# Layer 0 of a two-layer kernel: one multiply by C over two neighbouring PSUM banks instead of two over one bank each

## The reference, cut to what matters

```python
A = -jnp.exp(A_log[0])
dA = jnp.exp(delta[..., None] * A[None, :, None, :])
dBu = (delta * u)[..., None] * Bs[:, None, :, :]
...
_, states = jax.lax.associative_scan(comb, (dA, dBu), axis=2)
y = jnp.einsum('bdln,bln->bdl', states, Cs) + D_param[0][None, :, None] * u
```

## Time and profile before

| | us |
|---|---|
| median of 3 executions | 3519.16 |
| profiled execution, its time | 3515.45 |
| profiled execution, its span | 3513.4 |
| PE busy in the span | 3303.4 (94%) |
| DVE busy | 2848.3 (81%) |
| ACT busy | 2436.5 (69%) |
| POOL busy | 2366.1 (67%) |
| L1052 (`times_c`), 768 operations | 487.6 |

### The profile page before, as it was taken

One profiled execution on the slowest core, in us unless ns is written; L12 is line 12 of the kernel. 1 busy time (PEld: TensorE's weight loads), 2 busy tenths in 40 slices (PEclk: granted clock), 3 DMA queues, 4 the chain that ended last, 5 costly groups with the idle time before them and its releaser, 6 DMA issues. The chain is left out here.

```text
span 3513.4 us, 38815 instructions
## 1 busy us (share of the span) xinstructions
PE 3303.4 (94%) x10616; PEld 1690.2 (48%) x10616; DVE 2848.3 (81%) x4084; ACT 2436.5 (69%) x4194; POOL 2366.1 (67%) x1566
## 2 busy tenths in 40 slices
PE   5967999999999999999999999997989999999998
PEld 2422343434334343443433434342347877777887
DVE  7799999999999999999999999998733355565532
ACT  3688888888888888888888888886535565433211
POOL 3399999999999999999999999999800001022111
PEclk9987999999999999999999999998999999999999
DMA  9444555565555655555565555646442233366654
GB/s 381 152 106 98 142 150 145 149 168 140 155 143 151 165 148 152 145 150 155 141 168 139 160 140 152 168 119 186 108 117 69 63 99 107 121 212 212 213 185 157
DMA packets 213736, 529.89 MB, mean 151 GB/s; under 512 B 25144, under 2 KB 46328, under 8 KB 208272
## 3 DMA queue, kind: packets, MB, share of 16 engines
q1 hardware_dynamic: 170512, 376.39, 33.4%
q0 software_dynamic: 43008, 151.02, 20.0%
HBM read 346.17 MB, written 80.48 MB: 121 GB/s over the span
## 5 line engine op out<-in xcount | busy, mean ns | idle before, releaser
L554 PE MATMUL p_in<-xn,win_v 128*128 128x512 f32 (+1 forms) x2160 | 976.7, 600 | 50.6 <-ACT halo L825 30.5
L570 PE MATMUL p_op<-uy,wout_ring 128*128 128x512 f32 x2160 | 975.5, 601 | 23.6 <-DVE x_res L1083 23.5
L1018 POOL TENSOR_TENSOR g_ring<-du,bc 128x2048 f32<-128x2048 f32 x192 | 870.8, 4535 | 15.1
L1046 DVE TENSOR_TENSOR_SCAN p_da<-p_da,state,g_ring 128x512 f32<-128x512 f32 x672 | 827.4, 1277 | 42.4 <-issue 28.7
L1069 DVE SCALAR_TENSOR_TENSOR p_cv<-win_v,conv_w,p_cv 128x512 f32<-128x512 f32 x960 | 723.1, 753 | 47.5 <-ACT p_cv L883 26.5
L554 PEld LDWEIGHTS p_in<-xn,win_v 128*128 128x128 f32 x2160 | 402.9, 192 | 594.1 <-issue 592.4
L570 PEld LDWEIGHTS p_op<-uy,wout_ring 128*128 128x128 f32 x2160 | 404.8, 191 | 581.5 <-issue 543.5
L764 ACT ACTIVATE p_da<-delta,A 128x512 f32<-128x512 f32 x768 | 500.0, 683 | 12.8 <-ACT state L769 0.4
L1052 DVE TENSOR_TENSOR g_ring<-p_da,bc 128x512 f32<-128x512 f32 x768 | 487.6, 677 | 0.0
L1524 PE MATMUL banks<-x_split,w_split 128*128 128x512 f32 x1152 | 458.1, 398 | 12.6 <-DVE x_split L1727 6.7
L1526 PE MATMUL banks<-x_split,w_split 128*128 128x512 f32 x1152 | 450.0, 391 | 0.0
(11 more groups left out here) (250 smaller groups left out, 4176.1 us busy)
## 6 DMA issues: line engine op xcount, KB each, us to landing
g_ring<-g_ring POOLq DMA_DIRECT2D x192, 512.0 KB, 5.2
win_v<-in_win SPq DMA_DIRECT2D x192, 384.0 KB, 3.1
wout_ring<-wout_scratch SPq DMA_DIRECT2D x184, 384.0 KB, 4.1
x_ring<-x_scratch SPq DMA_DIRECT2D x192, 256.0 KB, 2.7
q_scratch<-q_ring POOLq DMA_DIRECT2D x96, 256.0 KB, 2.5
x_split<-q_scratch SPq DMA_DIRECT2D x96, 256.0 KB, 3.4
out<-x_ring POOLq DMA_DIRECT2D x96, 256.0 KB, 2.9
x_res<-in_x SPq DMA_DIRECT2D x90, 256.0 KB, 4.6
```

Source lines behind the costliest of these rows:

```text
L554: last = nc.tensor.matmul(bank_in(i)[:, 0:n], WR[:, i % NW, t, :], XN[:, t, off:off + n], start=(t == 0), stop=(t == XT - 1))
L570: last = nc.tensor.matmul(p_op[:], OR[:, e % NO, k - h * HALF, :], ucol(c * K + k), start=(k == 0), stop=(k == K - 1))
L1018: nc.gpsimd.tensor_tensor(G[:, i % NG], DU[:].unsqueeze(1).broadcast_to([P, NS, N]), BB[:], ALU.mult).then_inc(s_dbu, 1)
L1046: nc.vector.tensor_tensor_scan(bank, bank, G[:, i % NG, n, :], init, ALU.mult, ALU.add)\
```

## The change

`times_c` now takes a pair p of states instead of one state n. It waits for the second scan of the pair, reads both banks of `p_da` and two neighbouring parts of `CB`, writes two neighbouring parts of the `G` slot, and counts `s_cm` up by 2. The four calls in a slot become two. No other engine's waits or order change.

```diff
-                def times_c(i, n):
-                    vec.wait_ge(s_scan, NS * i + n + 1)
-                    vec.wait_ge(s_c[n // 2], 16 * (i // K + 1))
-                    nc.vector.tensor_tensor(G[:, i % NG, n], p_da[:, n % 2, :], CB[:, n], ALU.mult).then_inc(s_cm, 1)
+                def times_c(i, p):
+                    vec.wait_ge(s_scan, NS * i + 2 * p + 2)
+                    vec.wait_ge(s_c[p], 16 * (i // K + 1))
+                    nc.vector.tensor_tensor(G[:, i % NG, 2 * p:2 * p + 2], p_da[:], CB[:, 2 * p:2 * p + 2], ALU.mult)\
+                      .then_inc(s_cm, 2)
...
                         scan(a, 0)
                         scan(a, 1)
                         times_c(a, 0)
-                        times_c(a, 1)
...
                         scan(a, 2)
                         scan(a, 3)
-                        times_c(a, 2)
-                        times_c(a, 3)
+                        times_c(a, 1)
```

## The result

| | before | after |
|---|---|---|
| median of the executions, us | 3519.49 (4) | 3556.72 (4; 3553.14 to 3557.37) |
| span of the profiled one | 3513.4 | 3554.6 |
| idle time of VectorE's scans in the steady part | 14.4 | 3.1 |

The ratio is 1.0105, with an interval from 1.0091 to 1.012: 37 us slower. (The kernel before has one more execution here than where the forecast starts from, 3519.16.) The forecast was 3530, 11 us slower, with a range to 3545. The sign was right, and so was the view that VectorE becomes the pace; the price of a pair was too low by half, and a term of it was missing.

A forecast was written before the change was run, and what follows sets the result against it. The prediction took PE with its ScalarE answers to set 150 us a chunk in layer 0. Steady part 8.2, head 1.0 and tail 1.5 sum to 10.7 us, added to 3519.2 for a forecast of 3530, range 3516 to 3545.

The forecast's parts named there:

- the price of a pair: Layer 0, second scan to the operation behind the products: 1.16 us against 1.09, so VectorE loses 0.07 us a pair.
- What bounds the kernel: Layer 0's steady part: PE with its ScalarE answers sets 150 us a chunk; VectorE has about 1.0 us to spare.
- the cover: VectorE's idle time in layer 0's steady part, 14.4 us, about 1.0 us a chunk, which absorbs added VectorE time.
- The start: Wide product behind the second scan: starts 0.04 us after its end instead of 0.09 before, losing 0.13 us a pair.
- The length: Wide product on VectorE: 512 more columns cost 0.53 us, so it lasts 1.21 us.
- The deduction: Layer 0's steady part: 22.6 us of new VectorE time less 14.4 us idle time leaves 8.2 us.
- The head: Layer 0, 184 to 354 us: 28 pairs, 2.0 us, of which half is taken, 1.0 us.
- The tail: Layer 0, 2370 to 2511 us: 26 pairs by 0.07 make 1.8 us, taken as 1.5 us.
- PE keeps the pace: Rival: the wait behind a scan costs little or nothing, so PE sets the period; 3516 to 3519 us, chance 0.22.
- faster: Rival: 0.06 us a pair saved and the period follows VectorE; 3497 us, chance 0.07.
- The cover is not usable: Rival: VectorE's steady-part stalls come back in full, nothing is deducted; +26 us, 3545, chance 0.13.
- The wide product is dear: Rival: wide product costs two full durations and the wait, 0.22 us a pair; 3580 us, chance 0.04.

The follow-up runs named there:

- dose of 64 columns: Kernel before, with one extra VectorE product of 64 columns, used by nobody else, ahead of each tile's first scan; 3531.77 us, ratio 1.0033.
- step of 1: Changed kernel, with the wide product counting its semaphore up by 1 instead of 2 and the counts waited for halved; 3540.71 us, ratio 1.0055.
- dose of 192: Kernel before, with one extra VectorE product of 192 columns, used by nobody else, ahead of each tile's first scan; 3552.13 us, ratio 1.0095.
- wait alone: Kernel before, its narrow products of 512 columns kept, but both products of a pair wait for the pair's second scan; 3561.17 us, ratio 1.0116.
- C's wait hoisted: Changed kernel, with the wait for C's load moved ahead of the pair's first scan, leaving the wide product one wait; 3563.38 us, ratio 1.0121.
- one bank read twice: Changed kernel, but the wide product reads the second bank of p_da twice, leaving out the first and third state; 3554.45 us.

## Why the prediction was wrong, point by point

*What bounds the kernel.* Right. PE with ScalarE's answers set 150 us, VectorE had 1.0 us a chunk to spare. Periods against VectorE's added time bear it out, with the cover as the one constant:

| kernel | added a chunk | less 1.0 | period - 150.0 | mean of twelve chunks, less 150.1 before |
|---|---|---|---|---|
| dose of 64 columns | 12 x 0.135 = 1.6 | 0.6 | 0.4 | 0.6 |
| step of 1 | 24 x 0.085 = 2.0 | 1.0 | 0.9 | 0.9 |
| dose of 192 | 12 x 0.27 = 3.2 | 2.2 | 2.0 | 1.8 |
| the change | 24 x 0.14 = 3.4 | 2.4 | 2.3 | 2.2 |
| wait alone | 24 x 0.15 = 3.6 | 2.6 | 2.5 | 2.3 |

Over twelve chunks the rule gives a little too much for the three larger ones (by 0.2 to 0.4 us).

*The start: this step failed.* I took 0.13 us from L1083 behind L1076, the nearest row. A product that counts by 1 behaves just so: gap 0.034, 0.128 us later than before. The change also raised the semaphore's step to 2, which I listed in the diff and priced at nothing (beside the width I named only the scan waited for as what differs). With it the product lost the wait that it carries itself (L1083, my row, carries its own), and that added 0.056 us a pair, 18 us over 323 pairs. My upper bound of 0.26 for the start held the measured 0.18, but the range did not carry it through: 323 x 0.05 is 16 us, and nothing of that is covered once the cover is spent.

*The length: too short.* 1224 ns instead of 1210. About half of that is the wait on the neighbour: behind a tap, where it waits for nothing near, the wide product lasts 1217 ns in the mean. The slope of 1.04 ns a column was right (691, 825, 1158 and 1225 ns for 512, 640, 960 and 1024 columns, each waiting for the scan), and crossing a bank costs nothing. Together 0.14 us a pair, not 0.07.

*The deduction: right in form.* 323 x 0.14 - 14.4 = 31 us where I had 8.2. Doubling a price before a fixed cover is taken off made the rest nearly four times as large. The 25.9 us of the twelve chunks between the marks and 4.9 for the next one are this term.

*The head: too small. The tail: near.* 5.4 us in the head where I took 1.0. The price alone explains 28 x 0.14 = 3.9 there. More than that may be what two traces differ by: the first mark stands at 379.7 with C's wait hoisted, which costs more a pair than the change, at 382.4 with one bank read twice and at 384.6 in the change itself. In the tail the chain of one pair grew from 4.66 to 4.80 us, but several pairs wait for something else and kept their time, and in all it lost 2.4 us where I took 1.5. How much of the head's loss is the change's was not tested.

*The rivals.* "PE keeps the pace" and "faster" fell with the price of the wait (0.15 us a pair, measured alone). "The cover is not usable" would have shown stalls of 0.3 to 0.4 us left over; 14.4 us fell to 3.1. "The wide product is dear" asked for over 1250 ns and for a price at the banks, and got neither. That ScalarE's chain can carry a late product to PE I had named only as what is late next: it decided where ScalarE had to wait 0.65 us for the product.

## What to carry to other kernels

Fusing two operations saves one start (0.06 us here), but if the fused one must read what its direct neighbour wrote, it pays the wait that the second of the two had been hiding (0.13 us, and 7 to 16 ns of length): look in the queue for what stands between producer and consumer before fusing. When cover is deducted from a cost, put the bounds of the price through the deduction, because beyond the cover every hundredth counts in full, times hundreds of operations. And see to it that the wait on the neighbour stands in the operation itself: here that took a step of 1 and that wait named first.

## What the runs showed of the hardware that I had not expected

- A wait on the direct neighbour costs least when the VectorE operation carries it itself: the operation starts 0.034 us after the neighbour's end. In an instruction of the queue ahead of it, the same wait makes the start 0.090, 0.104 or 0.133 us late, by whether it stands second of two, alone or first of two there.
- A product with a semaphore step of 2 carried no wait of its own, so its start was 0.056 us later in the median (1024 columns). It makes no difference when the neighbour is not awaited: behind a tap it starts 0.09 us before the tap's end, with the step of 2 as with the step of 1.
- Of two waits, the one on the neighbour placed last costs 0.07 us on a narrow product (0.104 against 0.034) and 0.04 on the wide one with its step of 2 (0.133 against 0.090), for the same reason.
- Two memsets of one column cost no time that the timeline shows.
- A product of 32 columns, all in SBUF, lasted 181 ns at best, 499 in the median and 4255 at worst behind the wide product, while products of 64 and 192 columns ahead of the scans lasted 244 and 362 ns in the mean. The trace shows what the long ones waited for. All 204 products of 32 columns that lasted over 0.4 us began while a GpSimd operation was running, and each ended 0.044 to 0.055 us after that one's end:

```profile
1210.60 1.28 POOL L1014 TENSOR_TENSOR du<-delta,uy 128x512 f32<-128x512 f32 x1
1211.42 0.51 DVE L1057 TENSOR_TENSOR pad<-xproj_w 128x32 f32<-128x32 f32 x1
```

So these products, with both inputs in SBUF, were done only when the GpSimd operation that ran at their start was over. The wide product, which reads PSUM and SBUF, starts during such an operation in 368 of 384 cases of the same run and never lasts over 1226 ns. No run isolates what the two engines share.
